# A Mamba block and a top-2 expert layer on one core: seeded convolution and skip term, wider lead of the scan's products, first steps rearranged

## What is computed

```python
x = L0_attn_x                          # (2, 4096, 256)
xn = _layernorm(x)
x = x + mamba(xn, ...) + ffn(xn, ...)

# mamba: rms-normalise (norm_w); xz = xn @ in_proj_w.T; x_s, z = halves of 512
u = silu(causal depthwise conv(x_s), 4 taps, + conv_b)
x_dbc = u @ x_proj_w.T                 # dt_raw (16), B (16), C (16)
delta = softplus(dt_raw @ dt_proj_w.T + dt_proj_b)
dA = exp(delta * A);  dBu = (delta * u) * B       # 512 channels x 16 states
h = dA_t * h + dBu_t;  y_t = sum_s h * C_t        # over 4096 steps
y = (y + u * D_param) * silu(z)
return y @ out_proj_w.T + residual

# ffn: logits = x @ gate_w.T (8 experts); top-2 with gates by a masked softmax;
# per expert w2 @ (silu(w1 x) * (w3 x)), weighted and added for the two chosen
```

## Time and profile before

| | us |
|---|---|
| median of 3 runs (lowest, highest) | 2634.42 (2634.39, 2645.27) |
| profiled execution | 2637.98 |
| its span | 2636.2 |
| busy: VectorE / TensorE / POOL / ACT | 2350.0 / 2292.0 / 2035.6 / 1486.6 |
| start to first scan | 56.57 |
| units 0 to 35 | to 169.64 |
| routing and inverse | to 270.17 |
| rest of the short blocks 0 and 1 | to 341.23 |
| long blocks 2 to 29 | to 2455 |
| short blocks 30 and 31, tail | to 2636.2 |

### The profile page before, as it was taken

The page is one execution under the profiler, slowest core; times in us unless marked ns, Lnnn a source line. Parts: engine busy times, 40 slices in busy tenths (PEclk is TensorE's granted clock), DMA queues, the critical chain, the costliest instruction groups (busy, mean ns, idle before and its releaser), DMA issues. The chain is left out here.

```text
span 2636.2 us, 44811 instructions
## 1 busy us (share of the span) xinstructions
PE 2292.0 (87%) x14442; PEld 1989.8 (75%) x14442; DVE 2350.0 (89%) x3113; ACT 1486.6 (56%) x3049; POOL 2035.6 (77%) x1607
## 2 busy tenths in 40 slices
PE   3968689999999999999999899999998999998665
PEld 2965478888887888878888878888887878886554
DVE  7679899999898999899999989989898998989886
ACT  3850555656656565656655565565556556565442
POOL 3340588888888888888888888888888888888763
PEclk7868789999999999999999999999999999999776
DMA  6315035555555556555555555555555555552541
GB/s 212 105 57 179 29 98 162 165 167 156 156 163 157 156 161 174 158 159 160 149 169 155 163 169 161 156 160 153 160 159 171 159 158 161 150 152 59 94 89 35
DMA packets 271178, 379.24 MB, mean 144 GB/s; under 512 B 21492, under 2 KB 166516, under 8 KB 270948
## 3 DMA queue, kind: packets, MB, share of 16 engines
q1 hardware_dynamic: 240292, 332.26, 40.1%
q0 software_dynamic: 28480, 43.94, 9.7%
q10 hardware_dynamic: 2176, 0.18, 0.1%
HBM read 332.59 MB, written 52.10 MB: 146 GB/s over the span
## 5 line engine op out<-in xcount | busy, mean ns | idle before, releaser
L1138 DVE TENSOR_TENSOR_SCAN h<-DA,carry,h 128x512 f32<-128x512 f32 x600 | 764.7, 1276 | 47.1 <-POOL h L550 24.3
L1364 PE MATMUL HT<-ident,h 128*128 128x128 f32 x2912 | 474.8, 292 | 182.0 <-DVE W L1155 93.9
L1364 PEld LDWEIGHTS HT<-ident,h 128*128 128x128 f32 x2912 | 358.6, 150 | 286.2 <-issue 259.2
L550 POOL TENSOR_TENSOR h<-W,bbc 128x512 f32<-128x512 f32 x300 | 408.9, 1400 | 91.9 <-PE HT L1364 42.9
L550 POOL TENSOR_TENSOR h<-du,bbc 128x512 f32<-128x512 f32 x300 | 408.0, 1414 | 88.2 <-PE HT L1364 50.1
L1138 DVE TENSOR_TENSOR_SCAN W<-DA,carry,W 128x512 f32<-128x512 f32 x296 | 377.3, 1276 | 26.0 <-POOL W L550 13.2
L1155 DVE SCALAR_TENSOR_TENSOR W<-HT,cT,W 128x512 f32<-128x512 f32 x480 | 349.5, 728 | 1.4 <-PE HT L1364 1.3
L1155 DVE SCALAR_TENSOR_TENSOR yT<-HT,cT,yT 128x512 f32<-128x512 f32 x480 | 349.3, 728 | 0.0
L817 ACT ACTIVATE DA<-delta,alog 128x512 f32<-128x512 f32 x448 | 302.2, 685 | 29.5 <-DVE h L1138 18.4
L817 ACT ACTIVATE DA<-W,alog 128x512 f32<-128x512 f32 x448 | 302.1, 685 | 28.6 <-DVE h L1138 19.0
L1423 PE MATMUL G<-W,fill 128*128 128x256 f32 x1080 | 274.3, 400 | 0.0
(11 more groups left out here) (227 smaller groups left out, 4307.2 us busy)
## 6 DMA issues: line engine op xcount, KB each, us to landing
W<-in_w_T_dram SPq DMA_DIRECT2D x405, 512.0 KB
bbc<-b_dram SPq DMA_DIRECT2D x256, 256.0 KB
xraw<-in_x_dram SPq DMA_DIRECT2D x64, 256.0 KB, 2.9
xn_dram<-W SPq DMA_DIRECT2D x8, 1032.0 KB, 14.5
W<-in_x_dram SPq DMA_DIRECT2D x32, 256.0 KB, 6.5
moe_dram<-fill SPq DMA_DIRECT2D x32, 256.0 KB, 3.9
out_dram<-tmpA SPq DMA_DIRECT2D x32, 256.0 KB, 2.1
out_dram<-moe_dram POOLq DMA_DIRECT2D x32, 256.0 KB, 4.4
```

What stands on the lines that cost most here:

```text
L550: pool.tensor_tensor(h(g), du_pair[n // 2 % 2][:, k, :], bbc[:, g // 4 % BRING, :], ALU.mult).then_inc(s_dbu, 1)
L1138: i = dve.tensor_tensor_scan(h(g), DA[:, g % 2, :], h(g), carry[:, b, s, k:k + 1], ALU.mult, ALU.add)
L1364: i = pe.transpose(HT[:, g % 2, c * P:(c + 1) * P], src, ident[:, :])
```

## The change

- The convolution's last tap and the bias are written into PSUM by ACT, from the copied projection (`copy_xs`: scale `cw`, bias `cb`, two activations of 256 columns for each half). PE does three taps instead of four. `cwd` shrinks and is made on POOL, as are the scalings of xpT and outT.
- The skip term is written into PSUM by ACT (`seed_y`, u times half of D), and `y_mm` adds only the transposes. `dskip` is gone.
- `AHEAD` 8 and `GROUPS` 4: the products run up to 8 units ahead in long blocks (4 in short ones; `product_at`), on 16 h slots. `LEAD` 3 for the loads of B.
- The tables move: most of all z1 from unit 2 to 0, y0 from 4 to 3, gate_y1 from 7 to 9, the copies of the projection from 9 and 12 to 11 and 13, xs1 from 10 to 9, conv0 and conv1 share unit 11, and the second multiply of an expert tile (`MULT`) comes one unit later.
- Block 0's exp - 1, correction, delta and du run on VectorE. Of each pair of token tiles, the odd one is normalised on VectorE (`normalise_odd`).
- The two largest logits are found by two maxima over all tiles instead of 64 `max` instructions.
- For the last block the residual is written ahead into the bank G, the out matmuls run half by half behind the two gates, and the block's expert rows are loaded into SBUF and added by VectorE, so that only one store follows.

```diff
-    AHEAD = 4
-    GROUPS = 3
+    AHEAD = 8
+    GROUPS = 4
...
-    LEAD = 2
+    LEAD = 3
...
+        product_at = []
+        for g in range(UNITS):
+            first = U * first_of_block(g)
+            at = max(g - (AHEAD if is_long(g // U) else 4), first - 4 + (g - first) // 2 if is_long(g // U) else 0)
+            product_at.append(max(at, product_at[-1] if g else -1) if g > 3 else -1)
...
-        FRONT = {"normalise": 6, "transpose": 7, "copy_xT": 8, "xs0": 8, "copy_xs0": 9, "xs1": 10, "copy_xs1": 12,
...
-                 "x_proj": 17, "copy_xdbc": 18, "store_b": 19, "dt": 19, "abs": 20, "exp": 22, "ln": 23, "sp0": 24, "sp1": 25,
...
-        BACK = {"z0": -1, "tanh_z0": 0, "silu_z0": 1, "z1": 2, "tanh_z1": 3, "silu_z1": 4, "y0": 4, "gate_y0": 6, "y1": 5,
...
+        FRONT = {"normalise": 6, "transpose": 7, "copy_xT": 8, "xs0": 8, "copy_xs0": 11, "xs1": 9, "copy_xs1": 13,
...
+        BACK = {"z0": -2, "tanh_z0": 0, "silu_z0": 1, "z1": 0, "tanh_z1": 2, "silu_z1": 3, "seed_y0": 2, "y0": 3,
...
-        XT_UNITS = (4, 13, 18, 23, 30)
+        XT_UNITS = (3, 13, 19, 23, 30)
...
-        INDEX, GATHER = -5, -4
-        XT, XT_COPY, H1, H3, TANH, A2, MULT, Y, YO, SCATTER = 0, 1, 2, 3, 3, 4, 4, 5, 6, 8
+        INDEX, GATHER = -6, -5
+        XT, XT_COPY, H1, H3, TANH, A2, MULT, Y, YO, SCATTER = 0, 1, 2, 3, 3, 4, 5, 5, 6, 9
...
+                if g == END + 42:
+                    sp.wait_ge(s_sc, 16 * NTILES)
+                    sp.dma_start(xr_late[:, :, :], moe_dram[(NB - 1) * T:NB * T, :].rearrange("(t p) d -> p t d", p=P)).then_inc(s_moe, 16)
...
-            exp_ready(0)
-            w_minus_1(0)
-            correction(0)
-            make_delta(0)
-            make_du(0)
-            for g in range(AHEAD):
+            pool.wait_ge(s_id, 10)
+            pool.wait_ge(s_par, NPAR)
+            for c in range(CH):
+                i = pool.tensor_tensor(cwd[:, c, :, :], ident[:, :].unsqueeze(1).to_broadcast([P, TAPS - 1, P]),
+                                       cw[:, c, 0:TAPS - 1].unsqueeze(2).to_broadcast([P, TAPS - 1, P]), ALU.mult)
+            i.then_inc(s_made, 1)
+            for at, to, by in ((0, R, 0.5), (R, R + NS, 0.25), (R + NS, ROWS, 0.5)):
+                pool.tensor_scalar(xpT[:, :, at:to], xpT[:, :, at:to], by, 0.0, ALU.mult, ALU.add).then_inc(s_made, 1)
+            pool.wait_ge(s_outT, 16)
+            pool.tensor_scalar(outT[:, :, :], outT[:, :, :], 0.5, 0.0, ALU.mult, ALU.add).then_inc(s_made, 1)
+            for g in range(4):
...
-                if g + AHEAD < UNITS:
-                    make_dbu(g + AHEAD)
+                for u in range(g, min(g + AHEAD + 1, UNITS)):
+                    if product_at[u] == g:
+                        make_dbu(u)
...
-                act.copy(src[:, :, :], cb[:, 2 * q:2 * q + 2].unsqueeze(2).to_broadcast([P, 2, T])).then_inc(s_seed, 1)
+                for m in range(2):
+                    c = 2 * q + m
+                    i = act.activation(src[:, m, :], xs[:, c, HALO:HALO + T], ACT.Identity, bias=cb[:, c:c + 1],
+                                       scale=cw[:, c, TAPS - 1:TAPS])
+                i.then_inc(s_seed, 1)
+
+            def seed_y(n, q):
+
+                act.wait_ge(s_z, 2 * n + q + 1)
+                act.wait_ge(s_u, 2 * n + 2)
+                if n == 0 and q == 0:
+                    act.wait_ge(s_prep, NPREP)
+                for m in range(2):
+                    c = 2 * q + m
+                    i = act.activation((FA if q else FB)[:, m, :], u2(n)[:, c, :], ACT.Identity, scale=hdpar[:, c:c + 1])
+                i.then_inc(s_sy, 1)
...
-                for t in range(TILES):
-                    i = dve.max(top8[:, t, :], lg[:, t, :])
-                link(i)
-                vb = top8[:, :, 0:2].rearrange("p t w -> p w t").unsqueeze(3).to_broadcast(full)
+                one = [P, TILES, E]
+                count = scratch[7][:, 0:512]
+                equal_v = scratch[4].rearrange("p (w c) -> p w c", w=2)
+                onehot_v = scratch[6].rearrange("p (w c) -> p w c", w=2)
+                rest = scratch[7][:, 512:1024]
+                left = lg[:, :, :]
+                for w in range(2):
+                    link(dve.tensor_reduce(tops[:, w, :], left, AX.X, ALU.max))
+                    top = tops[:, w, :].unsqueeze(2).to_broadcast(one)
+                    link(dve.tensor_tensor(equal_v[:, w, :].rearrange("p (t e) -> p t e", e=E), left, top, ALU.is_equal))
+                    link(dve.tensor_tensor_scan(count, starts, equal_v[:, w, :], 0.0, ALU.mult, ALU.add))
+                    link(dve.scalar_tensor_tensor(out=onehot_v[:, w, :], in0=count, scalar=1.0, in1=equal_v[:, w, :],
+                                                  op0=ALU.is_equal, op1=ALU.mult))
+                    if w == 0:
+                        link(dve.scalar_tensor_tensor(out=rest, in0=onehot_v[:, 0, :], scalar=-3.0e38,
+                                                      in1=lg[:, :, :].rearrange("p t e -> p (t e)"), op0=ALU.mult, op1=ALU.add))
+                        left = rest.rearrange("p (t e) -> p t e", e=E)
...
+            def normalise_odd(i):
+
+                q = NT * i + 1
+                row = xall[:, q, 0:DM].rearrange("p (a k) -> p k a", k=2)
+                dve.tensor_scalar(row, row, at_col(rstd, q), at_col(nm, q), ALU.mult, ALU.add).then_inc(s_nrmv, 1)
...
-            dve.tensor_tensor(cwd[:, :, :, :].rearrange("p c k i -> p (c k) i"),
-                              ident[:, :].unsqueeze(1).to_broadcast([P, CH * TAPS, P]),
-                              cw[:, :, :].rearrange("p c k -> p (c k)").unsqueeze(2).to_broadcast([P, CH * TAPS, P]),
-                              ALU.mult).then_inc(s_prep, 1)
-            for at, to, by in ((0, R, 0.5), (R, R + NS, 0.25), (R + NS, ROWS, 0.5)):
-                dve.tensor_scalar(xpT[:, :, at:to], xpT[:, :, at:to], by, None, ALU.mult).then_inc(s_prep, 1)
...
+            dve.wait_ge(s_et, 1)
+            dve.tensor_scalar(tmpA[:, :, :], tmpB[:, :, :], 1.0, -1.0, ALU.add, ALU.add).then_inc(s_wm, 1)
+            dve.wait_ge(s_wm, 1)
+            dve.tensor_tensor(tmpA[:, :, :], tmpB[:, :, :], tmpA[:, :, :], ALU.subtract).then_inc(s_corr, 1)
...
+            dve.wait_ge(s_corr, 1)
+            dve.wait_ge(s_sp, 2)
+            dve.tensor_tensor(delta(0), delta(0), tmpA[:, :, :], ALU.add).then_inc(s_delta, 1)
+            dve.wait_ge(s_delta, 1)
+            dve.tensor_tensor(du(0), delta(0), u2(0), ALU.mult).then_inc(s_du, 1)
...
+                if g + NPRE < PAIRS:
+                    normalise_odd(g + NPRE)
...
+            n = NB - 1
+            dve.wait_ge(s_omm, NT * (n + 1))
+            dve.wait_ge(s_moe, 16)
+            dve.wait_ge(s_mamba, 16 * n)
+            dve.tensor_tensor(res, sums(n), xr_late[:, :, :], ALU.add).then_inc(s_res, 1)
...
-                for k in range(TAPS):
-                    i = pe.matmul(dst, cwd[:, c, k, :], xs[:, c, k:k + T], start=False, stop=(k == TAPS - 1),
+                for k in range(TAPS - 1):
+                    i = pe.matmul(dst, cwd[:, c, k, :], xs[:, c, k:k + T], start=False, stop=(k == TAPS - 2),
...
-                for m in range(2):
-                    c = 2 * q + m
-                    pe.matmul(dst[:, m, :], dskip[:, c, :], u2(n)[:, c, :], start=(m == 0), stop=False,
-                              skip_group_check=True)
...
-            for t in range(NT):
-                out_mm(NB - 1, t)
+            n = NB - 1
+            pe.wait_ge(s_oacc, NT * (n + 1))
+            for q in range(2):
+                pe.wait_ge(s_y, 2 * n + q + 1)
+                for t in range(NT):
+                    for c in (2 * q, 2 * q + 1):
+                        i = pe.matmul(sums(n)[:, t, :], zs[:, c, t * P:(t + 1) * P], outT[:, c, :], start=False,
+                                      stop=(c == CH - 1), skip_group_check=True)
+                    if q:
+                        i.then_inc(s_omm, 1)
...
```

## The result

The changed kernel takes **2443.55 us** (median of 4 runs, 2440.64 to 2446.11) beside 2635.89 us for the kernel before (2634.39 to 2645.27): the ratio is 0.9263, 95% interval 0.9238 to 0.9288. The forecast was 2494 us, range 2448 to 2585. The change gains as forecast, but more: the time lies 4 us under the range.

What follows compares the result with a forecast made beforehand. VectorE was taken to bound the deciding long blocks; gains of 109 + 7.7 + 6 + 4.6 + 5 (short blocks and units between) + 8.5 = 140.8 us gave 2497 profiled, 2494 us as median, range 2448 to 2585.

Steps and rivals of the forecast that it cites:

- The floor: Long blocks: VectorE's 69.3 us busy time a block cannot shrink, so only its 174.8 us of idle can be gained.
- 66 us of 174.8: Long blocks: VectorE idle time expected to remain, summed over causes of waiting, for a gain of 109 us.
- exponentials: Long blocks: scans waiting for ScalarE's exponential, 35.4 us before, expected at 42 because ScalarE has more to do.
- None of that is a gain by itself; it counts through lateness: Long blocks: TensorE's 97 us less work pays only by making it less late for VectorE.
- Rival (a): Long blocks: gaps refill, only the moved multiply and the products' lead pay; 2573 us, chance 0.20.
- Rival (c): Nearly every long-block gap goes and the clock holds in the first 36 units; 2435 us, chance 0.10.
- (b): Long blocks: ScalarE becomes the bound, skip seeds delaying exponentials in units 2 and 3; 2773 us at worst, chance 0.06.
- (d): TensorE's relief goes into waits for the same additions and terms outside cancel; 2630 us, chance 0.04.
- The start: Before the first scan: faster table operations with POOL idle put the first scan near 48.8 us, a gain of 7.7.
- Units 0 to 35: First 36 units: moved normalisation helps only at the high clock, plus a shorter convolution; gain 6 us.
- Routing: Routing's chain of VectorE operations: maxima over all tiles cut 17.8 us to 13.2, a gain of 4.6.
- Tail: End of kernel: earlier out matmuls and one store replacing the accumulating DMA; gain 8.5 us.

Runs made afterwards that it cites:

- the two runs that removed VectorE's gaps inside them: Changed kernel with the normalising passes ahead of the tanh: 2445.1 us; the same with the second half of y in unit 6: 2440.0 us.
- the kernel of the rows above: Changed kernel with the normalising passes ahead of the tanh and the second half of y in unit 4: 2442.2 us.
- the two runs meant to settle it: Changed kernel, normalising passes ahead of the tanh, y's second half in unit 4; expert tile at 23 moved to 24: 2504.1 us, or 19 to 18: 2487.8 us.

## Why the prediction was right and wrong

**The floor, the step that failed.** The step reads "so 69.3 us is a floor, and all that the stage can yield is the 174.8 us". It puts the gain in busy time at nothing. Busy time is the union of records, and a wait takes an overlap of 0.08 to 0.11 us out of it. Drawn out to no waits, the two lines give 1898 to 1908 us, 67.8 to 68.2 a block, an estimate. The fall from 347 to 66 waits was worth 27.4 us that the sum did not have. The second part of the miss is idle time: a gain of 109 us was forecast and 132.7 measured, 24 more. With either part alone the time would have lain inside the range, at some 2467 to 2470 us; the two together put it under. The Trainium skill ("Perfetto Trace Analysis", section Identifying the Most-Contended Engine) calls VectorE's occupancy a fair measure of the distance to its limit. Here it was 92% before, and 98% from 1000 to 1600 us after, but the busy time itself shrank with the waits, so the distance was larger than the idle time.

**What was left of the idle time.** I kept 66 us of 174.8; 44.5 were left. By cause, kept and measured: h3 3 and 0; the tanh 8 and 7.2; POOL 3 and 0; exponentials 42 and 29.6; the rest 10 and 7.7. So the causes came out right one by one, and the exponentials were mis-sized: I let them grow from 35.4 since ACT "has more to do", and the run without the seeds shows that its load costs nothing; what is left is the logarithm's chain, 0.58 us in each of 28 blocks, and 0.87 in every second. "No addition should wait" holds but for 3 waits, 1.4 us.

**TensorE's relief.** "None of that is a gain by itself; it counts through lateness": it counted everywhere, 39 to 57 us of the stage for 97 us of matmuls. I had walked TensorE with a slack of 3 us and its lateness back at zero within three units; the trace has 22 us without a gap, and the two runs that removed VectorE's gaps inside them gained nothing.

**Additivity.** The terms were priced by cause, and their sum came out near the idle time lost. As prices of the edits they would have been wrong: removing the h3 wait alone gives 13 us, not 47; the lead alone 4, not 34.5. So it was partly luck that the sum by causes came near: it holds because relief, order and lead came together. Rival (a), that the gaps refill, is what happens to the multiply alone and to the lead alone, the two that it had paying; the relief, which it had at nothing, paid most alone (39 us). The refilling did not happen to the three together. Rival (c), nearly every gap gone, came closest (2435), though its other half, the clock in the first 36 units, stayed away: 0.69 for 0.70 before. (b) and (d) did not occur.

**The start.** First scan at 50.28, forecast 48.8. The eight table operations behave as priced, and the first of them, 2.39 us in the earlier trace rows, is

```profile
44.17 0.27 DVE L1007 TENSOR_TENSOR W<-W 128x120 f32<-128x120 f32 x1
```

The moments ended at 41.1 us and not at 39.2, 1.9 us late where the whole missed by 1.5.

**Units 0 to 35.** The pitch of 3.31 us stayed, and the gain was 3.9 us for 6. That is no more than the same code differs by from one execution to another (113.1 and 108.9 us above), so what the moved normalisation gave there stays open; in the whole time it shows nothing. The Trainium skill's rule that spoke against the move ("GPSIMD Engine Reference", section 1, Specifications) shows in single rows: the normalisation at 51.59 us took 1.18 us beside POOL's product, against a median of 0.40. So reading every second column did not keep it clear of POOL. In the time of these units no loss shows.

**Routing.** 15.0 us from the first maximum to the start of the last product instead of 17.8, where 13.2 were forecast. The maxima and scans cost what they were priced (0.69 and 1.22); two operations ran beside POOL's products from 171.84 to 175.38 us and took

```profile
172.90 1.37 DVE L1070 TENSOR_SCALAR W<-W 128x512 f32<-128x512 f32 x1
174.30 1.63 DVE L1071 TENSOR_TENSOR W<-W 128x512 f32<-128x512 f32 x1
```

the second of them 0.69 without a product beside it, and ahead of the first maximum VectorE waits 0.70 us for the logits, which makes the stage's gain 2.1 us.

**Tail.** 12.7 us for 8.5. I took 5.3 us from the store to the end: 2.4 out of rows that held an accumulating DMA behind the store, and 2.9 that no row shows. The plain store needs 2.6 us in all, to 2444.4. TensorE, VectorE and the SP queue at the end:

```profile
2437.31 3.69 PE L1551 MATMUL G<-outT,zs 128*128 128x256 f32 x16
...
2441.04 0.69 DVE L1293 TENSOR_TENSOR tmpA<-G,xr 128x512 f32<-128x512 f32 x1 [2.98 <-PE G L1551]
...
2441.76 0.38 SPq L421 DMA_DIRECT2D out_dram<-tmpA  x1
```

The first out matmuls began with the second gate (2437.36 us) and so ran beside it, as forecast. All sixteen took 3.69 us for 5.41, and from their start to the end it is 7.1 us, not 11 to 12: 9 of the 12.7 us were gained there, for 4 to 5 forecast. In most of the experiments, with the same code there, the tail had a clock of 0.72 and took 15.5 us, so some 1.5 us of the gain goes with the higher clock of this execution.

## What to carry to other kernels

Busy time of an engine is no floor while waits stand in it: read the distance from start to start where nothing waits, and count the waits, since each costs its idle time and one lost overlap. Where several engines are within a few per cent of each other, a list of waits tells what could go if everything else kept up, not what one edit brings: here the multiply alone gave a quarter of its wait, and the three edits together 160 us where singly they gave 39, 35 and 4. Before moving work within a table, find the gapless stretch that ends at the wait, and follow what is queued behind the moved piece on its engine.

## What the runs showed of the hardware

TensorE's granted clock can fall inside a busy kernel behind a short wait. The stage before has 78 us at the low level and after 44. In the kernel of the rows above, the clock fell 0.4 to 0.7 us behind the end of the wait of 1.80 us in 12 of 28 blocks, and in the changed kernel, nearly the same program, in 3. So a wait on TensorE is sometimes paid a second time: the eight Y matmuls took 3.37 us for 1.89. What decides whether the clock falls behind a given wait is open; the two runs meant to settle it changed too much else.

VectorE's neighbouring instructions overlap by 0.08 us in the records where nothing waits, so a gap costs more than its length: 0.113 us of busy time each by the line through the twenty kernels.

A VectorE instruction beside a GpSimd product can take several times as long: 1.63 us for 0.69 (two inputs, 512 elements) and 1.18 for 0.40 (one strided input, 256 elements), and beside another of GpSimd's passes 2.39 for 0.27 (two inputs, 120 elements).
